# Embedding gathers of a DLRM tower on one core: waits for landings replaced by short writes on GpSimd

## Chip, cores and metric

One core of one Trainium2 chip runs the kernel. The metric is device time in microseconds (us), the median over the runs of one kernel.

## What is computed

The batch has 2048 samples. Each has 128 dense numbers and 26 ids, one for each of 26 tables with rows of 128 numbers. The reference, cut to what matters:

```python
e = jnp.stack([tbl_0[ids[:, 0]], ..., tbl_25[ids[:, 25]]], axis=1)      # (2048, 26, 128)
combined = jnp.concatenate([r_dense_features[:, None, :], e], axis=1)   # (2048, 27, 128)
inter = jnp.einsum('bnd,bmd->bnm', combined, combined)
z = jnp.concatenate([r_dense_features, inter[:, TRIU_I, TRIU_J]], axis=1)   # 351 pairs
h = jnp.concatenate([z, r_dense_features], axis=1)
h = jnp.maximum(h @ W_top1 + b_top1, 0.0)
h = jnp.maximum(h @ W_top2 + b_top2, 0.0)
y = h @ W_top3
```

## The kernel before, in words

The batch is cut into 16 tiles of 128 samples, two tiles (A and B here, `v` even and odd) to a round of 256. There are 8 rounds. Round 0 is `step((0, 0), None)`; rounds 1 to 6 come from the loop in `passes` (L202) and each of them also carries the dense layers of the round before; `last_step` (L488) is the last round, which has no next one to prepare for.

The vectors of a sample come in two ways. Ten of the tables (`SPREAD`) lie in SBUF, and their rows are picked by matmuls against one-hot matrices that VectorE builds (`compare`, L680, and `fetch`, L368, ten items a round). The other 16 are gathered by GpSimd: `gather_tile` (L272) issues 16 indirect DMAs for each tile, each of 128 rows of 512 bytes, so 256 in all. They land in `rows`, which has two buffers, one for A tiles and one for B tiles; its slot 0 is filled by SyncE with the dense numbers (L215).

The 17 slots of a tile form five groups of 3, 4, 4, 4 and 2 slots (L55), of which 2, 4, 4, 4 and 2 are gathered. Each group of each buffer has its own semaphore `gathered`. TensorE waits for the full count of a group (L327) and transposes its slots into PSUM (`transpose_rows`, L321, the matmuls of L334). There are two PSUM buffers `vec_ps`: ScalarE empties groups 0, 2 and 4, VectorE groups 1 and 3 (`copy_vecs`, L509), so group 4 of a tile can be transposed only once ScalarE has copied group 2 out, and group 3 once VectorE has copied group 1.

Then follow, for each tile, the products of all pairs (`dots`, L337, 64 small matmuls in each of two halves), whose results ScalarE and VectorE bring to SBUF (L571, L745), the split into a high and a low part (L577, L753) and the three dense layers (L414, L423, L430).

The order of work on each engine is written out by hand in its `step`. TensorE's order in rounds 1 to 6 (L442 to L486) is: A groups 0 and 1, item 0, A groups 2 to 4, layer 1 part 0, dots A, item 1, layer 1 parts 1 and 2, item 2, dots A, B groups 0 and 1, item 3, layer 1 part 3, B groups 2 to 4, then items 4 to 9 with dots B and layers 2 and 3 between them.

GpSimd has only the gathers once its few set-up instructions are done. Two kinds of waits order them:

- A tile's first gather waits until TensorE has transposed all of the tile two before it, whose buffer it takes (L278).
- Before each group GpSimd waits until the whole group before it has landed (L288), and inside a group of four it waits after the second until those two have landed (L295). With `AT_ONCE = 2` at most two gathers are under way at a time, and there are 8 pairs to a tile, 128 in all.

GpSimd's pool of descriptors in SBUF is set by `dynamic_dma_scratch_size=2048` (L868) in both kernels.

Of the kernel before, what the change touches and what calls it, by code (L numbers as in the profile page):

```python
# [5 lines left out]
P = 128  # L6
# [5 lines left out]
U32 = mybir.dt.uint32  # L12
# [1 line left out]
VECTORS = 27  # L14
SPREAD = (2, 8, 1, 5, 6, 9, 14, 18, 24, 26)

AT_ONCE = 2

ORDER = [f for f in range(VECTORS) if f not in SPREAD] + list(SPREAD)


def dlrm_tower(nc, dense, ids, ids_spread_rows, tables, w1, w1_laid, b1, w2, b2, w3, out):
# [31 lines left out]
    NR = N - len(SPREAD)  # L54
    groups = [list(range(a, b)) for a, b in ((0, 3), (3, 7), (7, 11), (11, 15), (15, 17))]  # L55
    NG = len(groups)
# [12 lines left out]
    with ExitStack() as ctx:  # L69
        def sb(name, shape, dt=F32):  # L70
            return ctx.enter_context(nc.sbuf_tensor(name, shape, dt))
# [4 lines left out]
        def sem(name):  # L76
            return ctx.enter_context(nc.semaphore(name))

        ident = sb("ident", [P, P])
        ones = sb("ones", [P, P])  # L80
        idx = [sb(f"idx{v}", [P, F], I32) for v in range(4)]
        rows = [sb(f"rows{u}", [P, NR, D]) for u in range(2)]
        vecs = sb("vecs", [P, 2, P, NP])
# [83 lines left out]
        idx_in = [sem(f"idx_in{v}") for v in range(4)]  # L167
        dense_in = [sem(f"dense_in{u}") for u in range(2)]
        gathered = [[sem(f"gathered{u}_{k}") for k in range(NG)] for u in range(2)]
        groups_begun = sem("groups_begun")  # L170
        gathers_resumed = sem("gathers_resumed")
        transposed = sem("transposed")
        vecs_by_act = sem("vecs_by_act")
        vecs_by_dve = sem("vecs_by_dve")
# [17 lines left out]
        def groups_of(tiles):  # L192
            return (tiles + 2) * NG

        def static(i):
            return isinstance(i, int)
# [72 lines left out]

        @block.gpsimd  # L270
        def _(pool):
            def gather_tile(i, v, first):  # L272
                pool.wait_ge(idx_in[v], i * 16 + 16)
                for k, group in enumerate(groups):
                    mine = [s for s in group if ORDER[s]]
                    if k == 0:

                        pool.wait_ge(transposed, i * (4 * NG) + groups_of(v - 1))  # L278
                    if k or not (first and v == 0):

                        if k:
                            ii, vv, kk = i, v, k - 1
                        elif v:
                            ii, vv, kk = i, v - 1, NG - 1
                        else:
                            ii, vv, kk = i - 1, 3, NG - 1
                        n = len([s for s in groups[kk] if ORDER[s]])
                        pool.wait_ge(gathered[vv % 2][kk], ii * (32 * n) + (vv // 2 + 1) * 16 * n)  # L288
                    pool.sem_inc(groups_begun, 1)
                    landed = i * (32 * len(mine)) + v // 2 * (16 * len(mine))  # L290
                    for n, s in enumerate(mine):
                        f = ORDER[s]
                        if n and n % AT_ONCE == 0:

                            pool.wait_ge(gathered[v % 2][k], landed + 16 * n)  # L295
                            pool.sem_inc(gathers_resumed, 1)
                        nc.gpsimd.indirect_dma_start(  # L297
                            out=rows[v % 2][:, s, :], out_offset=None, in_=tables[f - 1][:, :],
                            in_offset=bass.IndirectOffsetOnAxis(ap=idx[v][:, f - 1:f].bitcast(U32), axis=0),
                        ).then_inc(gathered[v % 2][k], 16)  # L300

            pool.memset(pick_f[:], 0.0).then_inc(picks_zero, 1)
            pool.wait_ge(picks_zero, 1)
            pool.affine_select(out=pick_f[:], in_=pick_f[:], compare_op=ALU.not_equal, fill=1.0, base=0,
                               pattern=[[-1, X], [0, P]], channel_multiplier=1).then_inc(picks_made, 1)
            for n, kt in enumerate((LONG, SHORT)):
                pool.iota(row_of_i[n][:], pattern=[[1, kt]], base=0, channel_multiplier=kt).then_inc(rows_counted, 1)
            pool.iota(mask_i[:], pattern=[[-1, JG]], base=0, channel_multiplier=1).then_inc(mask_begun, 1)
            pool.memset(ones[:], 1.0).then_inc(ones_set, 1)
            pool.wait_ge(ones_set, 1)  # L310
            pool.affine_select(out=ident[:], in_=ones[:], compare_op=ALU.is_equal, fill=0.0, base=0,
                               pattern=[[-1, P]], channel_multiplier=1).then_inc(ident_made, 1)
            for v in range(4):
                gather_tile(0, v, True)
            with pool.Fori(0, PASSES - 1) as i:
                for v in range(4):
                    gather_tile(i + 1, v, False)

        @block.tensor
        def _(pe):  # L320
# [561 lines left out]
```

## Time and profile before

| | us |
|---|---|
| median of 3 runs | 671.92 |
| lowest and highest | 666.92, 679.28 |
| the profiled execution | 669.0 |
| its span in the profile | 667.5 |

The profile takes one execution. Its span is the stretch between the first and last instruction that it shows, and the profiled execution's own time is 1.5 us longer. PE is TensorE, DVE VectorE, ACT ScalarE and POOL GpSimd. The busy time of a gather on POOL is the issuing alone; its landing comes later. The granted clock of TensorE is 1.0 at 2.4 GHz and 0.5 at 1.2 GHz. In a timeline a row is one instruction or several merged ones: start, duration, engine, line, operation, tiles, count, and in brackets the idle time before it and what ended it.

### The profile page before, as it was taken

What the parts mean: (1) busy time and instruction counts of PE and PEld (TensorE: products, weight loads), DVE (VectorE), ACT (ScalarE), POOL (GpSimd) and SP (SyncE); (2) the same over time, 40 slices, a digit from 0 to 9 for tenths busy, and PEclk for the clock granted to TensorE, in tenths of its full rate; (3) what the DMA queues carried; (4) which work ended last, traced back from release to release, by engine and by line L of the source; (5) the groups of instructions that cost most, each with busy time, mean ns of one, the idle gap of its engine ahead of it and who ended that gap; (6) DMA issues with size and microseconds to landing.
All of it is one profiled execution on the core that took longest, in us unless ns stands there. A gap on an engine that the chain in (4) does not pass through costs nothing. (4 is left out here: it accounts for less than half of the span.)

```text
span 667.5 us, 12112 instructions
## 1 busy us (share of the span) xinstructions
PE 509.0 (76%) x4385; PEld 453.6 (68%) x4385; DVE 363.1 (54%) x760; ACT 249.5 (37%) x750; POOL 250.6 (38%) x267
## 2 busy tenths in 40 slices
PE   2667797989798929996597939897498958965467
PEld 1556687878687918785586938786387948864356
DVE  5665687656366725665265645765266644723040
ACT  2221544364236413543135423554036333354041
POOL 3243433434343334343434344343434343434200
PEclk9766797789599967999698977999599976978589
DMA  8911121111111111111101111111111111111000
GB/s 205 251 28 28 29 65 30 32 30 32 30 31 32 28 28 34 32 35 28 36 26 34 29 31 30 35 30 32 29 32 29 32 28 33 28 29 28 20 1 1
DMA packets 16633, 26.45 MB, mean 40 GB/s; under 512 B 8126, under 2 KB 10694, under 8 KB 16572
## 3 DMA queue, kind: packets, MB, share of 16 engines
q0 software_dynamic: 8192, 16.79, 9.5%
q1 hardware_dynamic: 8380, 8.83, 5.4%
q8 instruction: 40, 0.66, 0.4%
q14 instruction: 21, 0.17, 0.1%
HBM read 25.60 MB, written 0.01 MB: 38 GB/s over the span
## 5 line engine op out<-in xcount | busy, mean ns | idle before, releaser
L297 POOL DMA_INDIRECT rows<-in_tbl,idx x256 | 246.8, 964 | 375.4 <-DMA rows<-in_tbl,idx 301.5
L687 DVE TENSOR_TENSOR onehot<-ids_ps,row_of 125x1024 fp32r<-125x1024 f32 (+1 forms) x162 | 200.5, 1274 | 127.8 <-PE ids_ps L365 123.1
L380 PE MATMUL fetch_ps<-onehot,t_hi 125*128 125x256 f32 x672 | 197.2, 320 | 30.6 <-DVE t_lo L710 24.1
L380 PE MATMUL fetch_ps<-onehot,t_lo 125*128 125x256 f32 x672 | 196.0, 319 | 0.0
L380 PEld LDWEIGHTS fetch_ps<-onehot,t_hi 125*128 125x128 f32 x672 | 143.9, 214 | 40.1 <-DVE t_lo L710 26.9
L745 DVE COPY_PREDICATED inter<-mask,dots_ps 27x64 f32<-27x64 int32 (+2 forms) x512 | 106.3, 208 | 92.8 <-ACT inter L571 78.1
L380 PEld LDWEIGHTS fetch_ps<-onehot,t_lo 125*128 125x128 f32 x672 | 143.5, 214 | 10.8 <-issue 3.8
L357 PE MATMUL dots_ps<-vecs 128*64 128x54 f32 x2048 | 136.1, 237 | 2.1 <-ACT vecs L512 2.0
L357 PEld LDWEIGHTS dots_ps<-vecs 128*64 128x64 f32 x2048 | 131.0, 151 | 9.1 <-issue 3.6
L571 ACT COPY inter<-dots_ps 27x64 f32<-27x64 f32 (+1 forms) x512 | 102.6, 200 | 86.9 <-PE dots_ps L357 70.9
L334 PE MATMUL vec_ps<-ident,rows 128*128 128x128 f32 x272 | 47.3, 307 | 110.3 <-DMA rows<-in_tbl,idx 96.0
L334 PEld LDWEIGHTS vec_ps<-ident,rows 128*128 128x128 f32 x272 | 32.5, 153 | 119.1 <-issue 86.0
L531 ACT COPY found<-fetch_ps 128x256 f32<-128x256 f32 x80 | 29.9, 373 | 144.7 <-PE fetch_ps L380 137.5
L512 ACT COPY vecs<-vec_ps 128x384 f32<-128x384 f32 (+2 forms) x48 | 28.7, 598 | 98.1 <-PE vec_ps L334 97.8
L512 DVE COPY vecs<-vec_ps 128x512 f32<-128x512 f32 x32 | 22.7, 711 | 58.6 <-PE vec_ps L334 58.3
L414 PE MATMUL mlp_ps<-x_hi,w_hi 128*128 128x256 f32 x160 | 44.1, 307 | 5.1 <-DVE x_lo L753 5.1
L414 PE MATMUL mlp_ps<-x_hi,w_lo 128*128 128x256 f32 x160 | 43.1, 300 | 0.0
L546 ACT COPY vecs<-found 128x1280 f32<-128x1280 f32 x16 | 39.5, 2474 | 0.6
L414 PEld LDWEIGHTS mlp_ps<-x_hi,w_hi 128*128 128x128 f32 x160 | 33.1, 207 | 5.2 <-issue 5.2
L414 PEld LDWEIGHTS mlp_ps<-x_hi,w_lo 128*128 128x128 f32 x160 | 33.5, 209 | 0.0
L584 ACT ACTIVATE h_sb<-mlp_ps,b_sb 128x256 f32<-128x256 f32 x32 | 15.2, 475 | 46.8 <-PE mlp_ps L414 42.1
L423 PE MATMUL mlp_ps<-h_sb,w_sb 128*128 128x256 f32 x128 | 32.0, 396 | 0.7 <-ACT h_sb L584 0.7
(44 smaller groups left out, 200.2 us busy)
## 6 DMA issues: line engine op xcount, KB each, us to landing
rows<-in_tbl,idx POOLq DMA_INDIRECT x256, 2.5
vecs<-in_tbl SPq DMA_DIRECT2D x8, 448.0 KB
rows<-in_r_dense_features SPq DMA_DIRECT2D x16, 64.0 KB
h_sb<-in_W_top_laid SPq DMA_DIRECT2D x2, 512.0 KB, 3.6
found<-in_tbl SPq DMA_DIRECT2D x1, 560.0 KB
h_sb<-in_tbl SPq DMA_DIRECT2D x1, 560.0 KB
w_sb<-in_W_top SPq DMA_DIRECT2D x1, 512.0 KB, 8.4
vecs<-in_tbl SPq DMA_DIRECT2D x8, 52.0 KB
```

Of the source, the lines that this page charges most:

```text
L297: nc.gpsimd.indirect_dma_start(out=rows[v % 2][:, s, :], out_offset=None, in_=tables[f - 1][:, :], in_offset=bass.IndirectOffsetOnAxis(ap= ...
L334: last = pe.transpose(vec_ps[k % 2][:, n * P:(n + 1) * P], rows[u][:, s, :], ident[:])
L357: last = pe.matmul(dots_ps[h * 64:h * 64 + 64, n, 0:PAIR], vs[:, b:b + 2, :].rearrange("p b f -> p (b f)"), vs[:, b:b + 2, 0:N], start=Tru ...
L380: last = pe.matmul(fetch_ps, part[0:KP, T0[k] + h * KH[k] + t, :], onehot[buf][h][0:KP, t, :], start=(h == 0 and t == 0 and part is t_hi), ...
L414: last = pe.matmul(mlp_ps[m % 2], w[:, jj, m * P:(m + 1) * P], x[:, jj, :], start=(at == 0), stop=(at == 3 * (JG + 1) - 1))
L423: last = pe.matmul(mlp_ps[m], w2_sb[:, k, m * P:(m + 1) * P], h1_sb[:, k, :], start=(k == 0), stop=(k == M1 - 1))
L512: copy(vecs[:, v % 2, :, a:a + n], vec_ps[k % 2][:, 0:n * P].rearrange("p (f b) -> p b f", f=n)).then_inc(done, 1)
L531: nc.scalar.copy(found[:, k, :], fetch_ps).then_inc(fetched, 1)
L546: nc.scalar.copy(vecs[:, t, :, NR:N], found[:, :, t * P:(t + 1) * P].rearrange("p k b -> p b k")).then_inc(placed, 1)
L571: nc.scalar.copy(inter_of(u, q, g, 0, count[g]), products_of(q, g * JG, count[g])).then_inc(inter_by_act, 1)
L687: dve.tensor_tensor(onehot[buf][h][0:KP, 0:kh], ids_ps[0:KP].rearrange("p (o r) -> p o r", o=1).to_broadcast([KP, kh, R]), rows_at[0:KP, h ...
L745: dve.copy_predicated(inter_of(u, q, g, a, n), mask[g * 32:g * 32 + N, a:a + n].rearrange("p (j s) -> p j s", s=1).to_broadcast([N, n, QS] ...
```

## The change

GpSimd no longer waits for any gather to land. The wait for the buffer (`transposed`) and the wait for the ids stay. Behind gathers 2, 4, ... 16 of each tile stands a `pause`: a wait for the writes of the pause before, an increment, and three memsets of 128 partitions by 125 numbers into `unread`, which nothing reads. TensorE's waits for `gathered` are as they were.

```diff
-AT_ONCE = 2
+        unread = sb("unread", [P, 3, 125])
...
-            def gather_tile(i, v, first):
+            PAUSES = NR // 2
+
+            def pause(i, v, n):
+
+                if not (static(i) and i == 0 and v == 0 and n == 0):
+                    pool.wait_ge(pauses_made, i * (12 * PAUSES) + 3 * (v * PAUSES + n))
+                pool.sem_inc(pauses_begun, 1)
+                for part in range(3):
+                    pool.memset(unread[:, part, :], 0.0).then_inc(pauses_made, 1)
+
+            def gather_tile(i, v):
                 pool.wait_ge(idx_in[v], i * 16 + 16)
+
+                pool.wait_ge(transposed, i * (4 * NG) + groups_of(v - 1))
+                pool.sem_inc(tiles_begun, 1)
                 for k, group in enumerate(groups):
-                    mine = [s for s in group if ORDER[s]]
-                    if k == 0:
-
-                        pool.wait_ge(transposed, i * (4 * NG) + groups_of(v - 1))
-                    if k or not (first and v == 0):
...
-                        n = len([s for s in groups[kk] if ORDER[s]])
-                        pool.wait_ge(gathered[vv % 2][kk], ii * (32 * n) + (vv // 2 + 1) * 16 * n)
-                    pool.sem_inc(groups_begun, 1)
-                    landed = i * (32 * len(mine)) + v // 2 * (16 * len(mine))
-                    for n, s in enumerate(mine):
-                        f = ORDER[s]
-                        if n and n % AT_ONCE == 0:
-
-                            pool.wait_ge(gathered[v % 2][k], landed + 16 * n)
-                            pool.sem_inc(gathers_resumed, 1)
-                        nc.gpsimd.indirect_dma_start(
-                            out=rows[v % 2][:, s, :], out_offset=None, in_=tables[f - 1][:, :],
-                            in_offset=bass.IndirectOffsetOnAxis(ap=idx[v][:, f - 1:f].bitcast(U32), axis=0),
-                        ).then_inc(gathered[v % 2][k], 16)
+                    for s in group:
+                        if ORDER[s]:
+                            f = ORDER[s]
+                            nc.gpsimd.indirect_dma_start(
+                                out=rows[v % 2][:, s, :], out_offset=None, in_=tables[f - 1][:, :],
+                                in_offset=bass.IndirectOffsetOnAxis(ap=idx[v][:, f - 1:f].bitcast(U32), axis=0),
+                            ).then_inc(gathered[v % 2][k], 16)
+                            if s % 2 == 0:
+
+                                pause(i, v, s // 2 - 1)
```

## Rows read from the trace of the kernel before

**Rows 1.** The page, busy time, share of the span and instructions of each engine

```profile
PE 509.0 (76%) x4385; PEld 453.6 (68%) x4385; DVE 363.1 (54%) x760; ACT 249.5 (37%) x750; POOL 250.6 (38%) x267
```

**Rows 2.** Waits, whole span: who waited for whom, us in total, times, longest

```profile
POOL rows L297 <- DMA rows<-in_tbl,idx: 301.5, 114, 8.8
...
PE vec_ps L334 <- DMA rows<-in_tbl,idx: 96.0, 24, 8.7
...
PE fetch_ps L380 <- DVE t_lo L710: 24.1, 10, 7.7
```

**Rows 3.** Timeline of POOL: start us, duration us, instruction, [idle before it <- releaser]

```profile
302.31 0.94 POOL L297 DMA_INDIRECT rows<-in_tbl,idx  x1 [2.62 <-DMA rows<-in_tbl,idx]
303.56 0.94 POOL L297 DMA_INDIRECT rows<-in_tbl,idx  x1 [0.31 <-issue]
307.04 0.94 POOL L297 DMA_INDIRECT rows<-in_tbl,idx  x1 [2.54 <-DMA rows<-in_tbl,idx]
```

**Rows 4.** Line L297 (the gathers), whole span

```profile
DMA to landing us min/median/max: 2.4/2.5/4.4
```

**Rows 5.** Timeline of PE, transposes of L334 in rounds 1 to 3 and the last

```profile
133.03 0.93 PE L334 MATMUL vec_ps<-ident,rows 128*128 128x128 f32 x7
...
140.03 0.44 PE L334 MATMUL vec_ps<-ident,rows 128*128 128x128 f32 x2 [2.33 <-ACT vecs L512]
160.32 0.98 PE L334 MATMUL vec_ps<-ident,rows 128*128 128x128 f32 x7
...
203.29 0.93 PE L334 MATMUL vec_ps<-ident,rows 128*128 128x128 f32 x7
...
229.38 0.98 PE L334 MATMUL vec_ps<-ident,rows 128*128 128x128 f32 x7
...
305.61 0.98 PE L334 MATMUL vec_ps<-ident,rows 128*128 128x128 f32 x7
...
320.12 1.11 PE L334 MATMUL vec_ps<-ident,rows 128*128 128x128 f32 x4 [8.59 <-DMA rows<-in_tbl,idx]
325.19 0.69 PE L334 MATMUL vec_ps<-ident,rows 128*128 128x128 f32 x2 [3.97 <-DMA rows<-in_tbl,idx]
...
353.99 0.93 PE L334 MATMUL vec_ps<-ident,rows 128*128 128x128 f32 x7
...
582.99 0.93 PE L334 MATMUL vec_ps<-ident,rows 128*128 128x128 f32 x7
...
606.03 0.99 PE L334 MATMUL vec_ps<-ident,rows 128*128 128x128 f32 x7
...
628.56 0.69 PE L334 MATMUL vec_ps<-ident,rows 128*128 128x128 f32 x2 [3.60 <-DMA rows<-in_tbl,idx]
```

**Rows 6.** Windows: stretch, length, busy PE, PEld, DVE, ACT, POOL; PEclk, DMA share, GB/s

```profile
324.00:327.00 3.00, 1.81 (x9) 1.81 (x10) 0.00 (x0) 0.60 (x1) 0.93 (x1) 0.50 0.11 27
```

**Rows 7.** Timelines of DVE and ACT beside B's groups, round 3 and the last

```profile
310.03 0.71 DVE L512 COPY vecs<-vec_ps 128x512 f32<-128x512 f32 x1
...
311.71 0.71 ACT L512 COPY vecs<-vec_ps 128x512 f32<-128x512 f32 x1
...
609.34 0.72 ACT L577 CAST x_hi<-inter 128x640 fp32r<-128x640 f32 x1
```

**Rows 8.** Timeline of POOL, first 17 us: memsets and first gathers

```profile
0.82 1.15 POOL L302 MEMSET found<- 10x1280 f32 x1 [0.29 <-POOLq L868]
...
3.74 0.22 POOL L309 MEMSET ones<- 128x128 f32 x1
...
4.98 1.15 POOL L297 DMA_INDIRECT rows<-in_tbl,idx  x1 [0.18 <-issue]
...
16.16 0.94 POOL L297 DMA_INDIRECT rows<-in_tbl,idx  x1 [8.78 <-DMA rows<-in_tbl,idx]
```

**Rows 9.** Timelines of DVE and POOL: a subtraction and the gather that started during it

```profile
321.87 0.81 DVE L753 TENSOR_TENSOR x_lo<-inter,x_hi 128x640 fp32r<-128x640 f32 x1
...
322.19 1.31 POOL L297 DMA_INDIRECT rows<-in_tbl,idx  x1 [0.31 <-issue]
```

More of the change, by code:

```diff
@@ L169, in dlrm_tower @@
         gathered = [[sem(f"gathered{u}_{k}") for k in range(NG)] for u in range(2)]
-        groups_begun = sem("groups_begun")
-        gathers_resumed = sem("gathers_resumed")
+        tiles_begun = sem("tiles_begun")
+        pauses_begun = sem("pauses_begun")
+        pauses_made = sem("pauses_made")
         transposed = sem("transposed")
@@ L274, in gather_tile @@
                 for k, group in enumerate(groups):
-                    mine = [s for s in group if ORDER[s]]
-                    if k == 0:
-                        pool.wait_ge(transposed, i * (4 * NG) + groups_of(v - 1))
-                    if k or not (first and v == 0):
[L281 to L286, printed above, removed]
-                        n = len([s for s in groups[kk] if ORDER[s]])
-                        pool.wait_ge(gathered[vv % 2][kk], ii * (32 * n) + (vv // 2 + 1) * 16 * n)
@@ L313, in _ @@
             for v in range(4):
-                gather_tile(0, v, True)
+                gather_tile(0, v)
             with pool.Fori(0, PASSES - 1) as i:
                 for v in range(4):
-                    gather_tile(i + 1, v, False)
+                    gather_tile(i + 1, v)
         @block.tensor
```

## The prediction, made before the changed kernel was run

> **What bounds the kernel now.** The page comes first: TensorE is busy for 76% of the span, nothing else for more than 68%, and GpSimd for only 38% [rows 1]. That looks like a TensorE kernel, but the shares don't say what a round waits for. The list of waits does: GpSimd waits 301.5 us for its own gathers to land, in 114 waits, and TensorE waits 96.0 us for gathered rows, in 24 [rows 2]. The third reading is GpSimd's timeline: a gather, 1.25 us later the next, and 3.48 us after that the first of the next pair, so a pair lasts 307.04 - 302.31 = 4.73 us [rows 3]. The landing takes 2.5 us from the start of the second gather [rows 4], so 2.5 - 0.94 = 1.56 us of GpSimd's idle 2.54 us are spent waiting for it, and the other 0.98 us are its restart behind the wait. The fourth is TensorE's own timeline. From the first transpose of round 1 at 133.03 to that of the last round at 582.99 lie six rounds, so (582.99 - 133.03) / 6 = 74.99 us a round [rows 5]. A round holds 16 pairs, and 74.99 / 16 = 4.69 us is the pair's period. So in rounds 1 to 6 GpSimd's chain of pairs sets the pace. TensorE catches up with it at one place: B's groups 3 and 4, where round 3 waits 8.59 and 3.97 us [rows 5].
>
> The start is different. Until about 70 us TensorE waits for the low parts of the tables (24.1 us in 10 waits), not for gathers [rows 2].
>
> **The gathers' waits go.** Each pair loses the wait for its landing, 128 times, and I take the restart to go with it (if it stays is a rival below). What remains of a pair on GpSimd is the first gather with its gap, 1.25 us, the second, 0.94 us [rows 3], the pause, and a gap before the next gather. The gap after an ordinary GpSimd instruction was 0.18 us once, ahead of the first gather [rows 8]; between gathers it is 0.31 us [rows 3].
>
> **The pauses come.** The trace shows no memset of 128 by 125. The nearest row is the memset of 128 by 128, 0.22 us [rows 8], and I take that: 3 x 0.22 = 0.66 us. From below the three could overlap almost wholly with what the engine does anyway, so nothing; from above, the memset of 10 by 1280 took 1.15 us [rows 8], which makes 3.45 us, and with a gap of 0.31 us ahead of each 4.4 us. The pause's wait is for the pause before, one pair (over 2 us) earlier, and ended long ago; behind it only the memsets and gathers of GpSimd itself are queued. The three increments and 128 more waits run in its sequencer, and I cost them at nothing while an instruction of the engine covers them; without that cover they lie within the 0.31 us gaps.
>
> A pair is then 1.25 + 0.94 + 0.31 + 0.66 + 0.18 = 3.34 us, and 16 of them 53.4 us. From the two ends it is 2.4 to 6.8 us, 38 to 109 us a round. What decides is the next bound: the pair stops mattering when 16 of them take less than TensorE's round.
>
> **What is late next: TensorE's round without waits for rows.** I cut it in three at the transposes.
>
> 1. A's first transpose to B's first. Round 1 had no wait for rows there: 160.32 - 133.03 = 27.29 us. It holds 2.33 us of another wait, for ScalarE, which must place the fetched vectors and empty `vec_ps` before A's group 4 [rows 5]. That wait stays. In round 2 the same part took 229.38 - 203.29 = 26.09 us [rows 5]. I take 26.9.
> 2. B's first transpose to its group 4. In round 3 this was 325.19 - 305.61 = 19.58 us [rows 5]. VectorE had emptied B's group 1 at 310.03 + 0.71 = 310.74, and ScalarE group 2 at 311.71 + 0.71 = 312.42 [rows 7]; group 2 didn't wait for rows worth mentioning and group 3 could follow at once. So group 4 could start at about 312.5, after 6.9 us.
> 3. B's group 4 to the next A. In round 3: 353.99 - 325.19 = 28.80 us [rows 5]. It began at the low clock: the granted clock was 0.50, the level of 1.2 GHz, from 324 to 327 us, behind the long wait for rows [rows 6]. If it is warm, half of about 4 us comes back: I take 26.8.
>
> The sum is 26.9 + 6.9 + 26.8 = 60.6 us against 74.99, so 14.4 us less, six times: 86.4 us. At 60.6 us a pair may take 60.6 / 16 = 3.79 us before GpSimd is the bound again; I expect 3.34, so it has some 7 us a round to spare. The buffer waits don't undo this: gathers for the next A may start at A's group 4 (7.0 us into the round: 140.03 - 133.03 [rows 5]), and 27 us later they are done; those for the next B start at about 34 us and are needed after 87.
>
> **The last round.** From B's first transpose to its group 4 it is 628.56 - 606.03 = 22.53 us [rows 5]. ScalarE's split ahead of its copy of group 2 ended at 609.34 + 0.72 = 610.06 [rows 7]; with a copy of 0.71 us, group 4 can start at 610.8, after 4.8 us: 17.7 us less. The tail behind it is a chain of TensorE, ScalarE and VectorE without gathers and stays 38.9 us; it starts at the low clock now, and may win up to 2 us, which I don't count.
>
> **The start.** Gathers are now issued while the table loads fill the DMA engines. The second pair used to wait 8.78 us and start at 16.16 [rows 8]; now some four more gathers compete with the first table. I charge 1 us, from 0 to 5. The first tile's rows are ready sooner, which gains nothing, since the tables decide.
>
> **The sum.** 86.4 + 17.7 - 1 = 103.1 us off the span of 667.5 makes 564.4, and 1.5 us around it 565.9 for an execution like the profiled one (669.0). The median of the runs shown is 671.92, 0.4% higher; that would add 2.5 us, about what the uncounted tail gives back. I predict **566 us**.
>
> **A lock between VectorE and GpSimd.** The gather that started 0.32 us into a subtraction of two SBUF tensors took 1.31 us instead of 0.94 [rows 9]. A round of the loop has two such subtractions (L753), which make under 1 us of GpSimd's spare 7, and I add nothing. The Trainium skill (SBUF — State Buffer, "Who interferes with whom") says that GpSimd is shut out of a shared port for the whole of a VectorE instruction in a two-port mode, and that two SBUF inputs conflict only with a GpSimd instruction that reads SBUF. The trace agrees as far as the gather, which reads its ids, stretched; no run here yet shows a memset beside VectorE. By the rule the memsets, which only write, would not stretch, and the sum stays; if it were otherwise and every pause met a subtraction, 0.37 us a pair makes 3.71, still under 3.79.
>
> **The rivals.**
>
> *GpSimd stays the bound, only faster.* The pair takes more than 3.79 us, because the restart of 0.98 us is needed anew after each pause: 3.34 - 0.18 + 0.98 = 4.14 us. A round is then 16 x 4.14 = 66.2 us and the time 566 + 6 x 5.6 = 600 us, with some of the waits for rows back at B's groups 3 and 4. For it: the restart is there behind every landing. Against: between two gathers with no open wait only 0.31 us pass, so the sequencer prepares the next one while the engine works.
>
> *The pause takes the wait's place, and the kernel gets slower.* Each memset takes as long as the one of 1.15 us, with gaps: 6.8 us a pair. From 4.69 us a pair upward the change loses. At 6.8 it adds 2.1 x 128 = 270 us: about 940 us. For it: that row is a memset of the same engine. Against: it has 1280 numbers to a partition, ten times as many.
>
> *TensorE's round is shorter or longer than three parts of different rounds say.* If the clock never falls, part 1 takes 26.1 and part 3 26.4: 59.4 us, so 559 us. If VectorE, which has 363.1 / 8 = 45 us of work to a round [rows 1], in 61 us rather than in 75, is late for one-hot items, and the clock falls at A's group 4 each time, 3 us a round come on top: 584 us. I count these into the forecast.
>
> *No change,* since something unseen has the same period: nothing in the waits supports it, because TensorE's waits for other engines are short.
>
> **Chances.** Forecast with its variants (550 to 590) 0.80; GpSimd the bound at 590 to 657 us 0.15; within 2% 0.03; slower 0.02. A measurement of this kernel can tell about 2% from no change. So faster 0.95, same 0.03, slower 0.02. The range of 8 in 10 reaches from 548 to 595 us.
>
> **What would show it.** GpSimd's timeline: pairs 3.2 to 3.5 us apart, three memsets of about 0.22 us each, then a gap; idle before L297 mostly for TensorE's transposes (the buffer), some 7 us a round. TensorE's waits for rows: from 96 us to under 10. Its rounds: 60 to 61 us. ScalarE as releaser of the transposes' waits, about 2.3 us a round. The granted clock near 1.0 behind B's group 4. The prediction is wrong if pairs are over 3.8 us apart, if gathers take much over 0.94 us with more of them under way, or if landings grow well past 2.5 us so that TensorE still waits for rows.

## The result, and the profile after

The changed kernel takes 774.88 us, median of 4 executions (774.4 to 775.69), against 669.42 us before (666.13 to 679.28): 1.16 times as long, with a 95% interval from 1.153 to 1.166. I had predicted 566 us. The page of the profiled execution:

```profile
span 774.2 us, 12584 instructions
...
PE 584.6 (76%) x4385; PEld 501.1 (65%) x4385; DVE 363.3 (47%) x760; ACT 247.9 (32%) x750; POOL 313.6 (41%) x651
...
PE   2678766687959778597876879778795977868967
...
POOL 8860817236270544507263180813627054450000
PEclk9555777795968869598786968879596886959898
```

TensorE still has its share of 76% [rows 1], but in a longer span, with more busy time (584.6 against 509.0 us): its granted clock was lower, 0.788 in the mean against 0.851. POOL now alternates between bursts and nothing. The waits, with their total, number and longest:

```profile
POOL rows L292 <- PE vec_ps L332: 248.0, 11, 28.5
DVE inter L743 <- ACT inter L569: 189.5, 39, 10.6
ACT inter L569 <- remote: 181.2, 26, 10.7
...
PEld fetch_ps L378 <- issue: 113.4, 119, 12.0
DVE onehot L685 <- remote: 96.4, 22, 9.0
```

Of [rows 2] the first two are gone: no wait for gathered rows is listed any more. TensorE stands still for 27.9 us in all ahead of its transposes, and ScalarE ends 22.2 of them, so its waits for rows can be 5.7 us at most. GpSimd waits for TensorE, to get its buffer back. New is the third line: ScalarE waits 181.2 us, ahead of its copies of the dot products, for something that the profile cannot name ("remote"). GpSimd itself does what the change says:

```profile
302.23 0.95 POOL L292 DMA_INDIRECT rows<-in_tbl,idx  x1 [0.16 <-issue]
303.48 0.94 POOL L292 DMA_INDIRECT rows<-in_tbl,idx  x1 [0.30 <-issue]
304.43 0.50 POOL L281 MEMSET unread<- 128x125 f32 x3
305.08 0.95 POOL L292 DMA_INDIRECT rows<-in_tbl,idx  x1 [0.16 <-issue]
```

A pair takes 305.08 - 302.23 = 2.85 us where [rows 3] had 4.73. The harm is on the other engines while such a burst runs. This is TensorE early in the burst from 258 to 280 us (start, duration, instruction, idle before it):

```profile
264.68 0.38 PE L378 MATMUL fetch_ps<-onehot,t_hi 125*128 125x256 f32 x1
265.29 0.28 PE L378 MATMUL fetch_ps<-onehot,t_lo 125*128 125x256 f32 x1 [0.23 <-issue]
265.41 0.29 PE L378 MATMUL fetch_ps<-onehot,t_hi 125*128 125x256 f32 x1
266.06 0.28 PE L378 MATMUL fetch_ps<-onehot,t_lo 125*128 125x256 f32 x1 [0.35 <-issue]
266.80 0.37 PE L378 MATMUL fetch_ps<-onehot,t_hi 125*128 125x256 f32 x1 [0.46 <-issue]
267.50 0.28 PE L378 MATMUL fetch_ps<-onehot,t_lo 125*128 125x256 f32 x1 [0.34 <-issue]
```

These matmuls wait for nobody ("issue") and still start up to 0.7 us apart, where 0.12 is their step (265.29 to 265.41). ScalarE in the same burst and in the next:

```profile
275.57 1.78 ACT L569 COPY inter<-dots_ps 27x64 f32<-27x64 f32 x8 [9.98 <-remote]
281.54 0.37 ACT L529 COPY found<-fetch_ps 128x256 f32<-128x256 f32 x1 [4.18 <-remote]
...
316.97 1.78 ACT L569 COPY inter<-dots_ps 27x64 f32<-27x64 f32 x8 [9.99 <-remote]
322.88 0.37 ACT L529 COPY found<-fetch_ps 128x256 f32<-128x256 f32 x1 [4.13 <-remote]
```

The last matmul of the half that ScalarE copies at 275.57 had started at 264.54. VectorE's compare at 281.53 needed ids that TensorE had multiplied at 269.02. The bursts' last gathers start at 279.3 and 320.6. The two waits of about 10 us end 3.7 us before that, still inside the burst; the four behind them, two of ScalarE and two of VectorE, end 2.3 us after it. Then TensorE in turn has run out of work (it stands still 7.34 us before 323.40, for ScalarE's copy), and its clock is down. In windows (length, busy PE, PEld, DVE, ACT, POOL; PEclk, DMA share, GB/s):

```profile
261.00:267.00 6.00, 4.75 (x58) 3.90 (x57) 2.30 (x3) 1.58 (x8) 5.06 (x11) 0.98 0.20 52
267.00:273.00 6.00, 4.56 (x18) 3.51 (x18) 1.59 (x9) 0.00 (x0) 5.06 (x11) 0.59 0.17 44
273.00:279.00 6.00, 3.78 (x13) 2.94 (x12) 1.68 (x8) 1.61 (x8) 5.03 (x11) 0.50 0.16 44
279.00:285.00 6.00, 4.44 (x20) 4.25 (x20) 2.35 (x2) 0.81 (x3) 1.44 (x4) 0.50 0.08 22
285.00:291.00 6.00, 6.00 (x82) 5.55 (x81) 2.89 (x5) 2.21 (x10) 0.00 (x0) 0.99 0.01 3
```

From 13 matmuls in 6 us to 82 as soon as the gathers are over; 64 of the 82 are the small ones of `dots`, but the matmuls of `fetch` too start 0.12 us apart again from 285.12 on. The DMA engines are busy for a fifth of the time: they are not full.

### The profile page after: what moved, and what is told of

It is laid out like the page before. It is cut to its first block, busy times and chain, and to the rows that moved or that the text cites. A ratio compares the mean times of both kernels' runs of the same rounds, so it can differ in the third digit from the quotient of the medians.

```text
span 774.2 us, 12584 instructions
## 1 busy us (share of the span) xinstructions
PE 584.6 (76%) x4385; PEld 501.1 (65%) x4385; DVE 363.3 (47%) x760; ACT 247.9 (32%) x750; POOL 313.6 (41%) x651
## 3 DMA queue, kind: packets, MB, share of 16 engines
q0 software_dynamic: 8192, 16.79, 8.2%
## 4 chain that ended last, share of the span: by engine, by line
PE 55%; another core or an unknown queue 18%; issue 11%; ACT 10%; DVE 5%; POOL 0%; ACTq 0%; DVEq 0%; POOLq 0%
PE fetch_ps L378 23%; PE dots_ps L355 12%; PE mlp_ps L412 12%; ACT inter L569 4%; PE mlp_ps L421 3%; ACT vecs L544 3%; PE vec_ps L332 2%; PE ids_ps L363 2%; DVE onehot L685 2%; ACT vecs L510 2%; DVE t_lo L708 2%; PE mlp_ps L428 1%; ACT found L529 1%; DVE inter L743 0%
## 5 line engine op out<-in xcount | busy, mean ns | idle before, releaser
L378 PE MATMUL fetch_ps<-onehot,t_hi 125*128 125x256 f32 x672 | 216.8, 342 | 98.6 <-ACT found L529 61.6
L378 PEld LDWEIGHTS fetch_ps<-onehot,t_hi 125*128 125x128 f32 x672 | 156.5, 233 | 122.2 <-issue 92.9
L378 PE MATMUL fetch_ps<-onehot,t_lo 125*128 125x256 f32 x672 | 216.4, 343 | 14.8 <-issue 14.4
L569 ACT COPY inter<-dots_ps 27x64 f32<-27x64 f32 (+1 forms) x512 | 102.1, 199 | 230.3 <-remote 181.2
L378 PEld LDWEIGHTS fetch_ps<-onehot,t_lo 125*128 125x128 f32 x672 | 156.4, 233 | 25.9 <-issue 20.5
L281 POOL MEMSET unread<- 128x125 f32 x384 | 63.9, 220 | 0.1
L332 PE MATMUL vec_ps<-ident,rows 128*128 128x128 f32 x272 | 42.8, 292 | 27.9 <-ACT vecs L510 22.2
L412 PE MATMUL mlp_ps<-x_hi,w_hi 128*128 128x256 f32 x160 | 54.2, 357 | 9.0 <-DVE x_lo L751 5.1
L412 PE MATMUL mlp_ps<-x_hi,w_lo 128*128 128x256 f32 x160 | 52.9, 349 | 4.6 <-issue 4.5
L332 PEld LDWEIGHTS vec_ps<-ident,rows 128*128 128x128 f32 x272 | 31.7, 148 | 33.8 <-ACT vecs L510 18.5
L412 PE MATMUL mlp_ps<-x_lo,w_hi 128*128 128x256 f32 x160 | 38.0, 359 | 13.1 <-issue 13.1
L421 PE MATMUL mlp_ps<-h_sb,w_sb 128*128 128x256 f32 x128 | 45.6, 522 | 1.9 <-issue 1.2
L412 PEld LDWEIGHTS mlp_ps<-x_lo,w_hi 128*128 128x128 f32 x160 | 32.3, 264 | 14.0 <-issue 13.9
L421 PEld LDWEIGHTS mlp_ps<-h_sb,w_sb 128*128 128x128 f32 x128 | 34.5, 281 | 9.0 <-issue 2.5
```

The lines of the kernel that those rows point to most:

```text
L281: pool.memset(unread[:, part, :], 0.0).then_inc(pauses_made, 1)
L332: last = pe.transpose(vec_ps[k % 2][:, n * P:(n + 1) * P], rows[u][:, s, :], ident[:])
L378: last = pe.matmul(fetch_ps, part[0:KP, T0[k] + h * KH[k] + t, :], onehot[buf][h][0:KP, t, :], start=(h == 0 and t == 0 and part is t_hi), ...
L412: last = pe.matmul(mlp_ps[m % 2], w[:, jj, m * P:(m + 1) * P], x[:, jj, :], start=(at == 0), stop=(at == 3 * (JG + 1) - 1))
L421: last = pe.matmul(mlp_ps[m], w2_sb[:, k, m * P:(m + 1) * P], h1_sb[:, k, :], start=(k == 0), stop=(k == M1 - 1))
L569: nc.scalar.copy(inter_of(u, q, g, 0, count[g]), products_of(q, g * JG, count[g])).then_inc(inter_by_act, 1)
```

## The experiments

They ran in five series, each on another chip, with the kernel before beside them: 677.43 us in the first (e1 to e4), 676.16 in the second (e5 to e8), 670.57 in the third (e9 to e12), 671.35 in the fourth (f1 to f4), 676.58 in the fifth (g1, g2). That a chip matters I understood only after the fourth. "Pair" below is the median distance from one pair of gathers to the next within a tile, from the trace. e1 to e12 ran once each, the runs of the last two series two or four times. The changed kernel itself was in none of the five series.

### First series: waits or pauses

**e1** is the kernel before with the pauses put in and its waits for landings kept:

```diff
+                        if s % 2 == 0:
+                            pause(i, v, s // 2 - 1)
```

> The kernel before with all its waits for landings, and the pauses added: a pause behind every second gather. Theory M (the pauses disturb: their writes or their increments hold TensorE's signals to the other engines back): the stalls of up to 10 us that ScalarE and VectorE have behind TensorE while a tile's gathers are issued appear here too, time above 720 us. Theories D (the gathers come too densely) and F (too many gathers are under way at once): the memsets hide in the 1.6 us of waiting, pairs stay 4.7 us apart, 665 to 685 us, and no such stalls.

674.73 us, pair 4.72. The pauses alone cost nothing that one execution beside one of before can show: they lie in the time that the landing takes anyway.

**e2** is the changed kernel without pauses (its call of `pause` is taken out).

> The changed kernel without the pauses: no landing is awaited and nothing is written, pairs about 2.5 us apart. Theory M: the stalls are gone, about 570 us. Theories D and F: the stalls stay, denser but over a shorter run of gathers (20 instead of 23 us a tile), 750 to 800 us.

561.21 us, pair 2.50: the densest burst, and no trouble in it. So I took the pauses for the culprit.

**e3** makes each pause four times over, each three writes waiting for the three before.

```diff
+                for turn in range(4):
...
+                    for part in range(3):
+                        pool.memset(unread[:, part, :], 0.0).then_inc(pauses_made, 1)
```

> The changed kernel with each pause made four times over (12 writes instead of 3, each three waiting for the three before), pairs about 4.8 us apart, as dense as before but with no landing awaited. Theory D: no stalls, GpSimd's chain bounds as before, 670 to 690 us. Theory M: four times the writes and increments, stalls worse, over 800 us. Theory F: since a landing takes 2.5 us and a pair 4.8, hardly more gathers are under way than before, so about 680 us too.

697.92 us, pair 5.02: GpSimd is the bound, and again nobody waits for an unnamed releaser. More pause did no harm beyond its own length, which spoke against my reading of e2.

**e4** is the kernel before with four gathers between two waits:

```diff
-AT_ONCE = 2
+AT_ONCE = 4
```

> The kernel before with AT_ONCE = 4: waits for landings only ahead of each group, no pauses, up to four gathers under way and then a gap of 2.5 us. A tile takes about 31 us on GpSimd. If short runs of dense gathers do no harm (theory D with a store that empties over some 5 us, since the stalls begin about 5 us into a tile's gathers): 580 to 620 us. If each burst costs (theory F, by the number under way): stalls inside each group of four, 650 to 750 us. Theory M: no pauses, so no stalls, 580 to 600 us.

563.07 us, also without trouble. No run of this series shows a stall, so none of them could tell one explanation of it from another; that the chip was not one that stalls came out only later.

### Second and third series: what in the pause does it

**e5** ends each pause with a wait for its own writes instead of beginning it with one for those before:

```diff
-                    pool.wait_ge(pauses_made, i * (12 * PAUSES) + 3 * (v * PAUSES + n))
...
+                pool.wait_ge(pauses_made, i * (12 * PAUSES) + 3 * (v * PAUSES + n + 1))
```

> The changed kernel, but each pause ends with a wait for its own three writes instead of beginning with one for those of the pause before, so GpSimd's sequencer can't run ahead of the engine by more than a pair. Theory R (the stalls need a sequencer that runs ahead through a queue of open gathers and memsets): no stalls, pairs about 3.3 us apart, 560 to 575 us. Theory B (what disturbs is the engine's own back-to-back work of gathers and memsets at this rate): stalls stay, above 700 us.

580.07 us, pair 3.66: almost cured, by a wait that makes GpSimd slower. Behind such a wait GpSimd stands still for 0.81 to 1.01 us before the next gather where the changed kernel has 0.16 (read from the trace of g1, the same program), so the restart of 0.98 us of the prediction's first rival is real, but only behind a wait for what is still running.

**e6** keeps one of the three writes, **e7** makes all three one number long (`unread[:, part, 0:1]`), **e8** has four increments by the sequencer and no write or wait, **e9** one such increment, **e10** three counted writes of 15 numbers, with no increment by the sequencer in the pause and its wait only once a tile.

> The changed kernel with one write of 125 numbers in a pause instead of three, wait and increment kept, pairs about 2.6 to 2.7 us apart. Theory R: the sequencer still runs ahead, stalls stay, above 680 us. Theory N (the number of counted instructions of GpSimd per time disturbs): a third of the writes, so much less, under 620 us.

> The changed kernel with all three writes, each of 1 number instead of 125 to a partition: the same instructions and increments, hardly any bytes. Theory R and theory N: stalls stay, above 700 us. Theory W (the bytes written to SBUF disturb TensorE's reads): stalls gone, 560 to 575 us.

> The changed kernel with four plain increments of a semaphore by the sequencer in a pause and no write. Theory N in its form for increments: stalls, above 650 us. Theories R and W and B: no memset, so as the run without pauses, 558 to 566 us.

> The changed kernel with one plain increment by GpSimd's sequencer in a pause, no wait and no write: 128 increments more than in the run without pauses and nothing else. Theory S (an increment of the sequencer's own among queued gathers is what disturbs): slow, 750 to 835 us, nearly as with four. Theory N (by the number of increments): a quarter of the extra of the run with four, about 630 us.

> The changed kernel with the three writes of a pause (of 15 numbers, each pause of a tile in its own place) counted by the engine, and no increment or wait of the sequencer's own except once a tile: pairs about 2.6 us apart. Theory S: no stalls, 558 to 568 us. Theory C (a change of instruction between gathers, of whatever kind, disturbs): 750 us and more.

They took 806.71, 826.3, 831.69, 808.58 and 805.3 us. Fewer bytes, fewer writes, no write at all: each is slower than the 775 us that the changed kernel took on its own chip. What they have in common is the shorter pair, 2.58, 2.52, 2.50, 2.50 and 2.57 us. The stall is there without a write (e8, e9) and with one increment as with four, so neither the writes nor the number of increments is the cause.

**e11** has twelve writes of 30 numbers, and the wait of the changed kernel:

```diff
-                for part in range(3):
+                for part in range(12):
```

> The changed kernel with twelve writes of 30 numbers in a pause instead of three of 125; the wait (for the pause before, so open when it is reached) and the increment are kept; pairs about 3.9 us apart. If an increment that the sequencer makes while it runs ahead disturbs at any rate: stalls, over 700 us. If it needs dense gathers too (theory S with a rate): no stalls and GpSimd the bound by a little, 575 to 600 us.

600.62 us. The pair is 3.13 us, 0.27 longer than in the changed kernel, and the time is 174 us shorter, with nine more writes in the pause. The two ran on different chips, though; on e11's own chip the nearest run is e10, 805.3 us at 2.57. ScalarE's unnamed waits ahead of those copies are down to 29.4 us, the longest 2.9:

```profile
281.88 0.95 POOL L292 DMA_INDIRECT rows<-in_tbl,idx  x1 [0.16 <-POOL unread L281]
283.13 0.94 POOL L292 DMA_INDIRECT rows<-in_tbl,idx  x1 [0.30 <-issue]
284.07 0.78 POOL L281 MEMSET unread<- 128x30 f32 x12
285.01 0.95 POOL L292 DMA_INDIRECT rows<-in_tbl,idx  x1 [0.16 <-POOL unread L281]
```

**e12** is e2 with one increment behind the eighth gather of a tile and one behind the sixteenth.

> As the run with one increment in a pause, but behind each eighth gather alone, two a tile, 32 in all. Theory S with a price for each increment: a quarter of the extra of one in each pause, 600 to 640 us. Theory T (the price is for the whole stretch of dense gathers once an increment stands in it): over 700 us.

813.29 us, with the same bursts as e2. Two instructions a tile could hardly cost 252 us, so e2 itself came under suspicion.

### Fourth series: was e2 repeatable?

**f1** is e2 word for word, **f2** is e4; **f3** has e12's two increments ahead of the tile's first gather, **f4** a single one behind its last.

> The changed kernel without its pauses, as e2, now in rounds. Theory Q (something that GpSimd handles between queued gathers holds back TensorE; the bare burst does not): every execution near 561 us, ratio to before 0.83 to 0.85. Theory B (a burst of 16 gathers can fall into either course by its phase to TensorE's work, and e2 was a lucky one): executions scatter, some between 750 and 830 us.

> The kernel before with AT_ONCE = 4, as e4, in rounds. Both theories: 563 us in every execution, ratio to before 0.83 to 0.86, since GpSimd stops after every fourth gather until they have landed. If it scatters, the number of gathers handed out at once is not what protects it.

> No pauses; the two increments of e12 stand together ahead of the tile's first gather, behind the wait for the transposes. Theory Q: no instruction stands between queued gathers, so 561 us as e2 (555 to 575). Theory B, or any added instruction or moved code on GpSimd (theory C): about 800 us in at least some executions.

> No pauses; one increment a tile, behind the sixteenth gather, so handed on by the sequencer while some ten gathers are still queued, but followed by no gather before the next tile's wait. Theory Q in its narrow form (an increment BETWEEN gathers does it): 561 us. Theory Q in its wide form (an increment behind queued gathers is enough, wherever it stands): about 800 us. Theory B and C: about 800 us too, and then f3 is slow as well.

f1: 815.13 us (811.96 to 821.82, 4 executions). f2: 612.86 (601.72 to 616.87), 0.90 times before (0.895 to 0.908). f3: 821.85, f4: 821.22. So theory Q is dead in both its forms, and e12 had told nothing of increments: on this chip the bare burst takes about 815 us in each execution. f2 and f1, side by side on one chip, also show that bounding the burst takes most of the loss away there: 613 us against 815. It isn't a lucky phase within a chip either, since f1's executions agree within 1.2% and f2's within 2.5%. e2 and f1 are one program on two chips. First the waits of e2, then those of f1:

```profile
ACT found L526 <- PE fetch_ps L375: 148.4, 73, 6.8
POOL rows L292 <- PE vec_ps L329: 126.8, 12, 18.5
```

```profile
POOL rows L292 <- PE vec_ps L329: 346.2, 12, 35.1
ACT inter L566 <- remote: 255.6, 27, 14.0
```

TensorE inside a burst of gathers in e2, and then in f1:

```profile
272.01 0.28 PE L375 MATMUL fetch_ps<-onehot,t_hi 125*128 125x256 f32 x1
272.13 0.28 PE L375 MATMUL fetch_ps<-onehot,t_lo 125*128 125x256 f32 x1
272.25 0.28 PE L375 MATMUL fetch_ps<-onehot,t_hi 125*128 125x256 f32 x1
```

```profile
291.23 0.37 PE L375 MATMUL fetch_ps<-onehot,t_hi 125*128 125x256 f32 x1 [1.55 <-issue]
293.39 0.37 PE L375 MATMUL fetch_ps<-onehot,t_lo 125*128 125x256 f32 x1 [1.78 <-issue]
295.51 0.37 PE L375 MATMUL fetch_ps<-onehot,t_hi 125*128 125x256 f32 x1 [1.75 <-issue]
297.62 0.37 PE L375 MATMUL fetch_ps<-onehot,t_lo 125*128 125x256 f32 x1 [1.74 <-issue]
```

A matmul every 0.12 us there, every 2.1 here, beside the same gathers 1.25 us apart. The traces differ in one more thing. e2's holds 7360 semaphore increments of the engines and 5004 landings, f1's 3575 and 1409: the rest was not recorded. That is also why "remote" stands where TensorE should, and why the page's row of landings has its 2.5 us in e2 but not in f1:

```profile
rows<-in_tbl,idx POOLq DMA_INDIRECT x256, 2.5
```

```profile
rows<-in_tbl,idx POOLq DMA_INDIRECT x256
```

By this mark the chips are of two kinds. The traces of the first and fifth series all hold about 5030 landings, those of the second to fourth 1119 to 3089. The changed kernel's holds 1916, so I count its chip as of the second kind. The trace of before has 3644 landings, where e1 with the same gathers has 5068, and it doesn't stall: the mark does not come from the stall alone. Nor is it there all the time: from the last round's first transpose, with no gather issued any more, to 2 us before the end, the traces of e2, f1 and the changed kernel hold 216 or 217 increments. The records are lost while gathers run. A series was one chip at one time, so what I call a kind of chip could also be a kind of occasion.

The gathers' own transfers are no slower on the second kind: their packets are busy for 11.3% of 559.7 us in e2 and 7.9% of 815.0 us in f1, so 63 and 64 us.

### Fifth series: the bytes, and the bounded version again

**g1** is e5 word for word. **g2** is e2 with half the bytes a gather; it leaves out half of each gathered vector:

```diff
-                                out=rows[v % 2][:, s, :], out_offset=None, in_=tables[f - 1][:, :],
+                                out=rows[v % 2][:, s, 0:D // 2], out_offset=None,
+                                in_=tables[f - 1][:, :].rearrange("r (h d) -> (r h) d", h=2),
```

> The changed kernel with each pause ending in a wait for its own three writes, as e5: pair 3.5 us. Theory D (gathers less than some 3 us a pair apart hold back TensorE, on some chips): 575 to 590 us, ratio to before 0.85 to 0.88, in every execution, since the pair is above 3 us. If e5 was a matter of luck: executions above 700 us.

> The kernel without pauses (e2, f1), but each gather takes rows of 64 numbers instead of 128: half of each vector is left out (zeroed once at the start) and the rows are other ones. The same number of gathers, increments and descriptors, 1.25 us apart; the bytes a microsecond are 0.57 of the changed kernel's. If bytes hold back TensorE: 555 to 600 us. If it is the gathers as such (issue, descriptors, increments): 800 to 825 us as f1. Should this call be like the first (e1 to e4), it would be 561 us either way; the number of increments recorded in the trace (7360 in e2, 3575 in f1) tells which.

g1: 561.58 us (560.48 to 562.17), 0.839 times before (0.830 to 0.848), pair 3.66 as in e5; the executions of before beside it lie between 666.58 and 678.35 us. g2: 559.71. But g1's trace holds 5020 landings and g2's 5048: this chip is of the first kind, where e2 takes 561 with all the bytes. So g2 tells nothing of bytes, and g1's 18.5 us less than e5 go with the chip.

Put together, pair against time:

| pair, us | first kind of chip | second kind |
|---|---|---|
| 5.02 | e3 698 | |
| 4.7 | before 677 and 677, e1 675 | before 671 to 676 |
| 3.8 (mean, four at once) | e4 563 | f2 613 |
| 3.66 | g1 562 | e5 580 |
| 3.13 | | e11 601 |
| 2.86 | | changed kernel 775 |
| 2.50 to 2.58 | e2 561, g2 560 | e6 to e10, e12, f1, f3, f4: 805 to 832 |

On the second kind the time first falls while the pair gets shorter, then turns. Each chip of this kind shows the turn by itself: 580 us at 3.66 and 807 at 2.58 (e5, e6), 601 at 3.13 and 805 at 2.57 (e11, e10), 613 with four at once and 815 at 2.50 (f2, f1). Where between 3.13 and 2.57 it comes on one chip, no run shows; the 775 us at 2.86 are of a chip of their own. That three chips of five, and the changed kernel's own, are of it is all that these runs say of how common it is.

## Why the prediction was wrong, by its own steps

**GpSimd's pair: right in kind, over-estimated.** I expected 3.34 us from 0.66 for three memsets and gaps of 0.31 and 0.18. The three together take 0.50 us, since they start 0.14 apart and last 0.22 each, and no gap stands ahead of them: 2.86 us. The restart of 0.98 us went with the wait, as assumed. The memsets weren't stretched: 215 to 230 ns over all 384. None of them met a subtraction of L751, but 18 met the subtractions of L708 at the start, which also read two tiles in SBUF, and took 216 to 223 ns; that agrees with what the Trainium skill (SBUF — State Buffer, "Who interferes with whom") says of a GpSimd instruction that only writes. The error of 0.48 us a pair looked harmless, because I held everything below 3.79 us to be equally good. On the second kind of chip it isn't: 3.13 us gave 601 us (e11, another chip), 2.86 gave 775.

**TensorE's round without waits for rows: the step that failed.** I took its three parts from rounds in which GpSimd had at most two gathers under way at a time, and assumed that the other engines would work as fast beside bursts of sixteen. From the first transposes, in us:

| | predicted | e2 (first kind) | changed kernel |
|---|---|---|---|
| round 1's | 134.0 | 137.66 | 157.35 |
| A to B, round 1 | 26.9 | 27.28 | 41.17 |
| B to the next A, round 1 | 33.7 | 33.64 | 51.07 |
| a round, mean of six | 60.6 | 59.77 | 92.20 |
| last round's to the end | 66.8 | 63.44 | 63.64 |

The second row is 164.94 - 137.66 and 198.52 - 157.35. Over the six rounds it goes from 23.8 to 27.3 in e2 and from 38.9 to 41.4 in the changed kernel, the third from 33.6 to 35.8 and from 50.9 to 52.9. The sum of the error is 23.3 at the start, 6 x 31.6 = 189.6 in the rounds and -3.2 at the end: 209.7 us, the whole of 774.2 - 564.4. In e2, on a chip of the first kind, both parts hold within 0.4 us in round 1 and the mean round within 0.9, B's group 4 starts 171.82 - 164.94 = 6.88 us behind its first transpose (6.9 predicted), and this kernel with still shorter pairs takes 561.21 us.

Of the three parts of the sum, the second held in the changed kernel too:

```profile
290.97 0.98 PE L332 MATMUL vec_ps<-ident,rows 128*128 128x128 f32 x7
297.91 0.44 PE L332 MATMUL vec_ps<-ident,rows 128*128 128x128 f32 x2 [0.99 <-ACT vecs L510]
343.90 0.98 PE L332 MATMUL vec_ps<-ident,rows 128*128 128x128 f32 x7 [1.80 <-issue]
```

That is 297.91 - 290.97 = 6.94 us. The third, from B's group 4 to the next A, took 343.90 - 297.91 = 45.99 us instead of 26.8 (44 to 46 over the rounds), and in the first it is the stretch behind A's group 4 that grew: 34.2 us in round 1, where 26.9 - 7.0 = 19.9 had been left. A burst of gathers starts right behind each of these two groups (258.01 and 299.36), since they free the buffer. The last round, in which no gather is issued, is equal in both columns (63.44 and 63.64): the loss lies where gathers are. Its 63.64 us begin at this row, 774.2 - 710.56:

```profile
710.56 0.93 PE L332 MATMUL vec_ps<-ident,rows 128*128 128x128 f32 x7
```

**The start.** I charged 1 us, at most 5. e2 paid 4.6 (137.66 against 133.03 [rows 5]); e1 and e4 on the same chip were at 135.98 and 131.63, so starts scatter by as much, and how much of the 4.6 is competition with the tables is not shown. The changed kernel paid 24.3, with ScalarE and VectorE waiting for the unnamed releaser as in the rounds.

**The clock.** I expected 1.0 behind B's group 4, and it is: TensorE has 1.00 from 297 to 309 us. It falls further on, to 0.50 from 273 to 285 us and from 309 to 315, once the burst has thinned out TensorE's work, and the half clock then makes the catching up slower. The fall goes with the stalls: one program has 0.938 in the mean without them (e2) and 0.779 with them (f1).

**What was right:** TensorE waits at most 5.7 us for rows; the transposes wait 22.2 us for ScalarE, in round 1 2.30 us at A's group 4 and 0.94 at B's; gathers stay at 961 ns. The last round's group 4 starts 4.82 us behind B's first transpose (4.8 predicted), and the tail behind it takes 36.9 us, the 38.9 less the 2 that I had not counted. None of the signs that I had named for being wrong came, neither pairs over 3.8 us nor gathers much over 0.94 nor waits for rows: the prediction was wrong in a way that it didn't watch for.

**The rivals.** GpSimd was not the bound, the pause did not take the wait's place, and the time is far from "no change". My slower rival asked for pairs above 4.69 us, and the kernel got slower with pairs of 2.86. None of them said that a faster GpSimd could hurt an engine with which it shares no wait, and 0.02 for slower left that no room. Nor could the trace of before have shown it: it has no burst. It has the marks of the second kind, though: 4.7 us of unnamed waits of ScalarE before those copies, no landing time for the dense inputs on its page, and 3644 landings.

**What stays open.** As far as five chips show, it needs a chip (or an occasion) of the second kind, and there the time follows how densely the gathers come, not the pause's writes, its increments or where they stand. Density alone is not isolated either: e5, e11 and f2 space the gathers by a wait, by more writes and by stops for landings, and no run only shifts them. Not shown is the way from the gathers to TensorE: their bytes, their descriptors, or the sixteen increments of each landing. Missing records of increments on the same chips, with increments that seem to arrive 10 us late, make a common path for increments and records plausible, and that is only argued. All executions here were recorded, and records are lost just while gathers run, so the recording may itself take part in the stall: whether the changed kernel is slow when nobody records is open, and it is the first thing to try. Whether the changed kernel itself takes about 565 us on a chip of the first kind wasn't tried; g1 and e2, above and below its pair, both took 561.

**A version that beats both.** Four gathers at once, or the changed kernel with the closing wait. The first gives 0.90 (interval above) on the second kind and 563 us against 677 in one execution on the first; the second 0.84 on the first and 580 us against 676 in one execution on the second.

## What to carry to other kernels

A wait that looks like pure loss can also be what spaces out a burst; before it is removed, ask what the whole chip does while the burst runs, and keep a bounded number under way. Here four gathers at once, or a wait every pair, kept the whole gain on the first kind of chip (563 and 562 us), and on the second 58 us of it (f2) and 96 us (e5) where the bare burst lost 144 (f1). A model of the next bound that is made of rows from the calm kernel holds for the calm case only, so it needs a rival in which the freed engine disturbs the others. And one execution on one chip is no control: a comparison that carries a theory is repeated beside its counterpart, or the chip is taken for the cause.

## What the runs showed of the hardware that I had not expected

- Beside gathers 1.25 us apart, matmuls that wait for nothing started 2.1 us apart on one chip and 0.12 on another (f1, e2).
- On one chip, 0.56 us more between pairs of gathers took 205 us off the kernel, though GpSimd had more to do (e11 against e10).
- The same chips lose records while gathers run: 1409 of some 5000 landings were in f1's trace, while the gathers' packets, all 8192 of them, are on its page. Where a trace names many releasers "remote" on one core, or its page lacks the landing times, its waits are to be read with care.
- Three memsets in a row start 0.14 us apart, twelve short ones take 0.78 us together; one behind a gather has no gap ahead of it. The next gather behind them starts after 0.16 us, but 0.8 to 1.0 us after them where GpSimd first waits for them (g1).
